# A fused decoder layer on one core: the middle layer's 16 dense steps become 14 pairs of a sorted token tile and a matrix

## The reference

```python
    def _L0_xattn_ref(hidden_states, token_ids, Wg, Wu, Wd):
        ...
        expert_ids = jnp.minimum(tid // tokens_per_expert, E - 1)
        out = jnp.zeros_like(hidden_states)
        for e in range(E):
            g = jax.nn.silu(jnp.einsum('bsd,fd->bsf', hidden_states, Wg[e]))
            u = jnp.einsum('bsd,fd->bsf', hidden_states, Wu[e])
            y = jnp.einsum('bsf,df->bsd', g * u, Wd[e])
            out = jnp.where((expert_ids == e)[..., None], y, out)
        return out
```

## Time and profile before

| | |
|---|---|
| median of 3 runs | 572.67 us (572.64 to 573.87) |
| the profiled execution's own time | 574.22 us |
| span of its trace | 572.3 us |
| TensorE busy | 510.2 us, 89% |
| VectorE busy | 424.0 us, 74% |
| ScalarE busy | 289.0 us, 50% |
| GpSimd busy | 201.8 us, 35% |
| mean granted clock of TensorE | 0.956 of full |

### The profile page before, as it was taken

One profiled execution on the slowest core, in us unless ns is written; L12 is line 12 of the kernel. 1 busy time (PEld: TensorE's weight loads), 2 busy tenths in 40 slices (PEclk: granted clock), 3 DMA queues, 4 the chain that ended last, 5 costly groups with the idle time before them and its releaser, 6 DMA issues.

```text
span 572.3 us, 11500 instructions
## 1 busy us (share of the span) xinstructions
PE 510.2 (89%) x3245; PEld 446.9 (78%) x3246; DVE 424.0 (74%) x1046; ACT 289.0 (50%) x794; POOL 201.8 (35%) x233
## 2 busy tenths in 40 slices
PE   7799999999999999999999979998877998796590
PEld 6688898998998988989989967897746886574380
DVE  6589988989889889898898787568846666341138
ACT  3566666656566566656565635444323443242250
POOL 3427604415215135053151005450074645606200
PEclk9999999999999999999999989998898999878596
DMA  7251212203102112011039409992023544424222
GB/s 195 89 145 55 65 30 56 64 1 80 39 27 64 27 37 64 18 55 37 0 105 354 167 0 289 302 292 74 1 83 117 160 146 131 128 93 130 73 92 101
DMA packets 59488, 57.10 MB, mean 100 GB/s; under 512 B 4080, under 2 KB 57152, under 8 KB 59328
## 3 DMA queue, kind: packets, MB, share of 16 engines
q1 hardware_dynamic: 56016, 48.16, 28.2%
q0 software_dynamic: 3168, 8.42, 5.3%
q10 hardware_dynamic: 272, 0.13, 0.1%
HBM read 46.21 MB, written 18.87 MB: 114 GB/s over the span
## 4 chain that ended last, share of the span: by engine, by line
PE 64%; DVE 18%; issue 10%; ACT 6%; POOL 1%; DVEq 1%; ACTq 0%; POOLq 0%
PE bank L768 12%; PE bank L769 12%; PE bank L770 12%; PE bank L942 12%; PE bank L950 6%; DVE rmax L1345 3%; DVE qk_lo L1337 3%; DVE nmax L1349 3%; PE bank L848 3%; ACT qk_hi L1145 2%; ACT prob L1153 2%; PE bank L946 2%; DVE pT_lo L1377 2%; PE bank L1056 2%; PE bank L774 1%
## 5 line engine op out<-in xcount | busy, mean ns | idle before, releaser
L1153 ACT ACTIVATE prob<-bank,nmax 128x256 f32<-128x256 f32 x128 | 59.5, 470 | 108.7 <-DVE nmax L1349 108.7
L585 POOL TENSOR_TENSOR w_lo<-st_c,w_hi 128x512 fp32r<-128x512 f32 x32 | 41.3, 1291 | 193.2 <-ACT w_hi L1116 193.2
L942 PE MATMUL bank<-moe_w,xT 128*128 x256 | 72.0, 407 | 3.7 <-DVE xT L1561 3.6
L1442 DVE TENSOR_TENSOR hid<-bank,sg 128x128 f32<-128x128 f32 x64 | 18.6, 291 | 59.0 <-ACT sg L1235 27.3
L1337 DVE SCALAR_TENSOR_TENSOR qk_lo<-bank,b_col,qk_hi 128x512 fp32r<-128x512 f32 x64 | 47.9, 748 | 16.1 <-ACT qk_hi L1145 15.3
L942 PEld LDWEIGHTS bank<-moe_w,xT 128*128 128x128 f32 x256 | 49.3, 204 | 12.2 <-issue 6.0
L768 PE MATMUL bank<-hT_hi,w_lo 128*128 128x512 f32 x128 | 52.8, 413 | 5.5 <-DVE qk_lo L1337 2.9
L1345 DVE TENSOR_REDUCE rmax<-bank 128x2 f32<-128x512 f32 x64 | 43.9, 686 | 13.8 <-PE bank L770 13.7
L769 PE MATMUL bank<-hT_lo,w_hi 128*128 128x512 f32 x128 | 50.7, 396 | 0.0
L770 PE MATMUL bank<-hT_hi,w_hi 128*128 128x512 f32 x128 | 50.4, 394 | 0.0
L667 POOL DMA_INDIRECT x_in<-h_dram,source x32 | 32.1, 1004 | 48.2 <-DVE source L1525 28.5
(11 more groups left out here) (213 smaller groups left out, 1558.9 us busy)
## 6 DMA issues: line engine op xcount, KB each, us to landing
y_dram<-ysb SPq DMA_DIRECT2D x64, 128.0 KB
moe_w<-in_w_gate SPq DMA_DIRECT2D x8, 512.0 KB, 8.4
moe_w<-in_w_up SPq DMA_DIRECT2D x8, 512.0 KB, 7.7
moe_w<-in_w_down SPq DMA_DIRECT2D x4, 1024.0 KB, 8.5
st_c<-in_wq_codes SPq DMA_DIRECT2D x16, 128.0 KB
st_c<-in_wk_codes SPq DMA_DIRECT2D x16, 128.0 KB
st_c<-in_wv_codes SPq DMA_DIRECT2D x8, 256.0 KB
st_c<-in_wo_codes SPq DMA_DIRECT2D x8, 256.0 KB
```

The costliest lines, as they stand in the source:

```text
L942: mm = pe.matmul(o, xT_of(kt), w, start=kt == 0, stop=kt == KT - 1)
L1153: ex = act.activation(prob[:, i % 4, qt, :], bS[i % 2][:, qt * S:(qt + 1) * S], ACT.Exp, bias=nmax[:, i % 2, qt:qt + 1], scale=SCALE, accu ...
```

## The change

The tokens of each half are sorted by their matrix. A sorted half is cut at its tile borders (128, 256, 384) and where the matrix changes (up to three places), which makes 7 segments, 14 in both halves; each is a pair of one 128-token tile and one matrix, with a 0/1 column `seg_mask` for the rows that belong to it.

- TensorE ranks the tokens in the last attention group (`token_ranks`), GpSimd works out each token's place (`places`) and the segments (`segments`). The mask tiles are gone.
- When the final output tiles are in, GpSimd scatters the rows of `x_acc` to their sorted places in `xs_dram` (`scatter`, 8 indirect DMAs), and SP loads them back. LN(1, 0) therefore starts after the reload, and its parts stand behind the attention's last slots on every engine. The expert weights' loads stand behind these loads on SP.
- A pair: ScalarE copies the tile's high and low parts to `h_seg` (in `pT_lo`), TensorE multiplies by the matrix whose address a register gives, ScalarE takes the silu, VectorE multiplies by mask and z in one instruction, TensorE turns the result, ScalarE and VectorE split it, TensorE multiplies, VectorE adds the sum to the tile of `x_acc` that a register names. There are two buffers of each. LN(1, 1)'s transposes stand between pair 6 and pair 7.
- The root of three of the norms is a power on GpSimd instead of a square root on ScalarE.
- Each token's origin goes the same way (`os_dram`), and at the end GpSimd scatters the output rows with 8 indirect DMAs instead of SP's four stores.

```diff
+            for half in range(NH):
+                sp.wait_ge(d_xs[half], 16 * HT)
+                ts = slice(half * HT, (half + 1) * HT)
+                sp.dma_start(x_acc[:, ts, :], xs_dram.rearrange("(t p) d -> p t d", p=P)[:, ts, :]).then_inc(d_xa[half], 16)
+
             sp.wait_ge(v_w, 4 * G + 1)
+            sp.wait_ge(p_seg, 1)
...
+            def scatter(half):
+
+                pool.wait_ge(p_dest, 1)
+                for t in range(half * HT, (half + 1) * HT):
+                    if t % 2 == 0:
+                        pool.wait_ge(v_w, Plan(G - 1).w_done_count(t // 2, True))
+                    pool.indirect_dma_start(out=xs_dram, out_offset=bass.IndirectOffsetOnAxis(ap=dest[:, t:t + 1], axis=0),
+                                            in_=x_acc[:, t, :], in_offset=None).then_inc(d_xs[half], 16)
...
+            pool.wait_ge(d_origin, 16)
+            for t in range(NT):
+                pool.wait_ge(v_cmb, combined(t))
+                pool.indirect_dma_start(out=out_rows, out_offset=bass.IndirectOffsetOnAxis(ap=origin[:, t:t + 1], axis=0),
+                                        in_=x_acc[:, t, :], in_offset=None).then_inc(d_out, 16)
...
             def pre(n):
 
-                half, e, ft = routed(n)
-                wait(pe, v_t, n - 3)
+                pe.wait_ge(a_copy, n + 1)
+                wait(pe, v_t, n - 1)
                 for kt in range(KT):
-                    mm = mm3(Z_BANKS[n % 4][:, :], cT_hi[:, e, kt, ft * P:ft * P + P], cT_lo[:, e, kt, ft * P:ft * P + P],
-                             hT_hi[:, kt, half * HALF:(half + 1) * HALF], hT_lo[:, kt, half * HALF:(half + 1) * HALF],
-                             kt == 0, kt == KT - 1)
+                    mm = mm3(Z_AT[n % 2][:, 0:D], h_seg[:, n % 2, kt * P:kt * P + P], h_seg[:, n % 2, (KT + kt) * P:(KT + kt) * P + P],
+                             kind_part(cT_hi, n, kt), kind_part(cT_lo, n, kt), kt == 0, kt == KT - 1)
                 mm.then_inc(t_z, 1)
...
+            for n in range(NSEG + 2):
...
+                if n == SEGS:
+                    mid(n - 1)
+                    post(n - 2)
+                    ln_tensor(pe, 1, 1, ENDS[1])
+                    post(n - 1)
                     pre(n)
...
+            def routed_product(n):
+
+                dve.wait_ge(a_z, n + 1)
+                wait(dve, t_turn, n - 1)
+                dve.scalar_tensor_tensor(out=gm[:, n % 2, :], in0=gact[:, n % 2, :],
+                                         scalar=seg_mask[:, half_of(n), n % SEGS:n % SEGS + 1],
+                                         in1=Z_AT[n % 2][:, 0:D], op0=ALU.mult, op1=ALU.mult).then_inc(v_t, 1)
```

More of the change, by code:

```diff
@@ L888, in _, with load_kinds @@
             over_groups(pe, body)
-            def zero(half):
-                for yb in ENDS[half]:
-                    pe.matmul(yb[:, :], zeros[:, :], zeros[:, 0:1].to_broadcast([1, HALF]), start=True, stop=True)
+            at = [pe.alloc_register(f"at{i}") for i in range(STEPS)]
+            def load_kinds(w):
+                apart(pe)
+                pe.reg_load(at[w % 2 * PACK:w % 2 * PACK + PACK],
+                            seg_expert[0:1, :, :].rearrange("p h i -> p (h i)")[:, w * PACK:(w + 1) * PACK])
@@ new lines, in body, with load_segments @@
+                    if pl.last and i == 4:
+                        dve.wait_ge(p_bounds, 1)
+                        for half in range(NH):
+                            ins = dve.max(sorted_b[:, half, :], bounds[:, half, :])
+                        ins.then_inc(v_sorted, 1)
+            over_groups(dve, body)
+            at = [dve.alloc_register(f"row{i}") for i in range(STEPS)]
+            def load_segments(w):
+                apart(dve)
+                dve.reg_load(at[w % 2 * PACK:w % 2 * PACK + PACK],
+                             seg_row[0:1, :, :].rearrange("p h i -> p (h i)")[:, w * PACK:(w + 1) * PACK])
@@ new lines, in routed_sum @@
+            def routed_sum(n):
+                row = dve.snap(at[word(n) % STEPS], min_val=0, max_val=(NT - 1) * D)
+                dve.wait_ge(t_y, n + 1)
+                wait(dve, v_y, n)
+                here = x_acc[:, :, :].rearrange("p t d -> p (t d)")[:, bass.ds(row, D)]
+                apart(dve)
+                dve.tensor_tensor(here, y_at(n), here, ALU.add).then_inc(v_y, 1)
+            norm = {(n, half): ln_vector(dve, n, half, x_acc) for n, half in LN_KINDS[2:]}
+            dve.wait_ge(d_xa[0], 16)
@@ L1422, in _ @@
-            statistics, variances, reciprocals, rows = ln_vector(dve, 2, 0, x_acc)
-            between = {4: lambda: ln_low(dve, 1, 1, ENDS[1]), 12: lambda: add_routed(0), 13: statistics, 14: variances}
-            for n in range(RSTEPS):
-                if n >= 1:
-                    routed_low(n - 1)
-                dve.wait_ge(p_gm, n + 1)
-                dve.tensor_tensor(gm[:, n % 4, :], Z_BANKS[n % 4][:, :], gact[:, n % 4, :], ALU.mult).then_inc(v_t, 1)
-                if n in between:
-                    between[n]()
@@ new lines, in _ @@
+            for n in range(NSEG):
+                routed_product(n)
+                if n >= 1 and n != SEGS:
+                    routed_low(n - 1)
+                if n == SEGS - 1:
+                    routed_low(n)
+                    ln_low(dve, 1, 1, ENDS[1])
+                    routed_sum(n - 2)
+                    routed_sum(n - 1)
+                    routed_sum(n)
+                elif n >= 2 and n not in (SEGS, SEGS + 1):
+                    routed_sum(n - 2)
+                beside(n)
@@ L1437, in _ @@
+            routed_low(NSEG - 1)
+            routed_sum(NSEG - 2)
+            routed_sum(NSEG - 1)
+            dve.wait_ge(v_y, NSEG)
+            for part in norm[2, 1]:
                 part()
@@ L1544, in _ @@
             own(dve.memset(xT_all[:, :, ROWS * SLOTS:(ROWS + 1) * SLOTS], 0.0))
-            at = [dve.alloc_register(f"row{i}") for i in range(STEPS)]
             def load_rows(word, first):
```

425 lines of the change are left out of this document (300 added, 125 removed).

## The result

The changed kernel takes **585.2 us** (median of four runs, 583.0 to 588.1) against 572.8 of the kernel before on the same chip: 1.0215 times, with a 95% interval of 1.0167 to 1.0264, so slower. Its profiled execution took 584.37 us with a span of 582.5; before it was 574.22 and 572.3.

What follows compares the result with a forecast made beforehand. TensorE, busy 89% of the span, was taken to set the middle layer's pace. Middle layer -6.5, root +0.3, end +1.6 gave -4.6 us; taken off the 572.67 median: 568.0 us, range 560 to 576.

Steps and rivals of the forecast that it cites:

- The end: At the kernel's end, eight GpSimd scatters replace four stores, so the output lands later: +1.6 us (range 1.2 to 2.4).
- The sign that the prediction named for being wrong here: At the kernel's end: the last scatter landing over 4 us after the last combination would show the forecast wrong.
- The rule weighed in the prediction: For scatter landings: a GpSimd DMA costs about 2.0 us plus bytes over 436 GB/s; 0.2 us less at each place.
- What is queued behind: Expert weights starting 3.3 us later and eight number scatters precede the first row gather, at 409 us: costs nothing.
- The root: In the last norm, the root comes from GpSimd instead of ScalarE: 0.3 us more.
- The round trip: Before the middle layer's pairs, rows go through DRAM and back; first product ends at about 350.9, 1.9 us later.
- The token ranks: In the last attention group, eight tiny matmuls beside a full TensorE: taken as 0.7 us.
- The pairs: In the middle layer, TensorE takes 1.9 us a pair; products 0 to 6 take 12.9 us, the second half's stretch 13.6.
- half to half: In the middle layer, from product 6 to the second half's first product: 7.0 us instead of one interval.
- the rival of half clock through all the pairs: In the middle layer, TensorE stays at half clock, a pair takes 3.1 us: 581.7 us, slower; chance 0.12.
- The expert stage: Behind the router, it should move as a block; its waits may land elsewhere by up to 4 us either way.
- the hand-offs: In the middle layer, each pair's six engine crossings set the pace, 2.6 us a pair: 574, slightly slower; chance 0.12.

Runs made afterwards that it cites:

- the end alone on the kernel before: The kernel before with its four plain stores at the end replaced by eight GpSimd scatters by plain row numbers: 586.5 us, 1.0215 times the kernel before.
- the first control: The changed kernel, with GpSimd reading the bound of each of its 32 result gathers one at a time: 582.5 us, 1.0181 times the kernel before.
- with sums in PSUM: The first control with VectorE keeping each tile's running combination sum in PSUM, on the faster chip: 1.0075 times the kernel before.
- the run with the drain: The first control with one GpSimd drain added behind its last result gather, in idle time, on the faster chip: 1.0040 times the kernel before.

## Why the prediction was wrong

**The step that failed is "The end", +1.6 us (range 1.2 to 2.4).** From last combination to end it has 4.15 us; the trace has 19.2. The 15 too few are the whole miss of the span: forecast -4.6 us, measured +10.2. They are two things. About 7.5 are the drain: the end was costed to the landing, and not to the engine's last instruction, which no view shows. The rest, some 7.5, are seven scatters in a row: the step took 1.00 us for a scatter from one that ran beside no combinations, and let six of eight go out beside VectorE. Adding the scatters alone to the kernel before cost 12.8 us (586.5 against 573.75 on its chip), and taking them out of the changed kernel's end brought it to 0.984. The sign that the prediction named for being wrong here, a last scatter that lands over 4 us after the last combination, came: it lands 11.2 us after it. The rule weighed in the prediction was only about a landing, and one that bears on the tail was left out. By the Trainium skill, "SBUF — State Buffer", section "SBUF: two separate sides", GpSimd and VectorE share a port pair as an exclusive lock, and a DMA issued by GpSimd starves for descriptors while VectorE holds it in a mode that uses both ports. Of an operation with two SBUF inputs it says that it takes the lock only against a GpSimd operation that reads SBUF, and it doesn't say that a DMA starves by that. The runs here show that a scatter, which does read its row numbers from SBUF, waits: 7.12 and 9.94 us beside such operations, 0.97 beside the others.

**"What is queued behind", at nothing,** also failed, for the weights that now end later and for the number scatters. It put the first row gather at 409; it came at 411.39, though the statistics were 2.8 us earlier than forecast. The reason given, that both are over ahead of that gather, was right; what they do to the engines and transfers beside them was not asked. With both there the stretch to the first row gather is 26.8 and 28.3 us at the low clock and 27.3 and 27.9 at the full one; without one of them it is 25.2 and 25.6 at the low clock and 23.4 at the full one. So together they cost the router between 1 and 4.5 us, and next to the reload the number scatters cost 6.

**The root, +0.3**: variance to the step behind the root takes 1.29 us instead of 0.65, so it costs 0.6.

**The round trip** came out at the forecast end, in part by luck. The first product ends at 350.88 (350.9), 1.9 us later than before, as forecast. But the reload was issued at 334.64 and in by 338.5, 2.4 us ahead of the forecast 340.9: the tile that the scatters wait for was ready at 330.6 and not at 332.2, and the 2.4 us of a landing run from the scatter's start, where the sum added its 2.5 behind the scatter's end. The norm did not start then. Its statistics stand behind the addition of W(1,3) on VectorE, which ends at 339.97, so VectorE's order set the start at 339.89, 1.0 ahead of the sum, and not the landing. Behind it the way to the first product took 11.0 us and not 10.0. The token ranks cost nothing visible.

**The pairs**: half to half 7.02 us (7.0), but products 0 to 6 in 11.2 us instead of 12.9 and 7 to 13 in 10.8 instead of 13.6. Short intervals are 1.05 to 2.07, long ones 3.18 and 3.31. TensorE's part was sized too large: intervals of 1.63 and 1.58 at full clock stand where 1.9 was forecast, so register operations cost nothing that shows, and the granted clock, 0.50 from 348 to 354, was 1.00 from 356 to 367 and from 374 on. Behind product 13 it took 4.2 us to the statistics instead of 2.5; LN(2, 0)'s transposes, 1.0 us of TensorE, stand ahead of the last turn. Together 384.10 instead of 386.9, so the middle was right in kind and worth 2.8 us more. The granted clock over 345 to 385 is 0.84, and the rival of half clock through all the pairs didn't come.

**The expert stage** moved as a block, 2.2 us shorter, within the 4 us allowed. The two rivals on the slower side, TensorE's clock and the hand-offs, both lay in the middle layer; neither came, and none looked at the tail.

## What to carry to other kernels

Follow the end of a kernel engine by engine to its last instruction: a GpSimd that issues the last transfer also drains there, here 0.082 us for every transfer since its last drain, and an explicit drain in idle time takes most of that away. Before moving a store from SyncE to GpSimd, ask what VectorE does meanwhile; here running sums in PSUM kept it out of GpSimd's way. Small scatters can delay the transfers beside them even where the engine that issues them has nothing else to do: let an index travel in its row.

## What the runs showed that I had not expected

- In the end alone on the kernel before, VectorE's operations are 0.48 us each, and a scatter waited out all of them for 9 us: GpSimd never got in between two.
- The kernel before takes 573 us on one kind of chip and 539 on another, and it is the expert stage: from first row gather to first combination 134 to 141 us on one, 106 to 107 on the other. The stages ahead of it take the same, as two such profiles show (last statistics at 381.95 in the first control, 382.13 with sums in PSUM). TensorE from 460 to 510 us in the first control and in the run with the drain (length, busy us, granted clock, DMA share, GB/s):

```profile
460.00:510.00 50.00, 42.36 (x196) 0.93 0.40 120
```
```profile
460.00:510.00 50.00, 49.99 (x247) 1.00 0.59 170
```

With the drain, on the faster chip, TensorE is never idle there and at full clock; in the control both are lower, with less data moved. Which comes first, the lower clock or the late transfers, stays open.
- What ScalarE waited for in the router ("remote") stays open: only what must be under way for it is shown, the number scatters by two profiles and the weights by one.
